# Second layer's experts: rows gathered per tile from a table in memory instead of 64 scatters into slots

## The chip, the cores and the metric

The kernel runs on one core of a Trainium2 chip. The metric is the device time of one execution in microseconds, as the median of the runs. Times inside the execution are read from a trace of one profiled execution, in microseconds from the start of its span.

## The reference, cut to what matters

The whole kernel is a chain of six layers over 16 images of 16x16 positions with 128 channels, which are 4096 tokens of 128 numbers. The change lies in the fourth of them, a mixture of 16 experts of which each token chooses two. Its hidden values are averaged over the tokens of an expert before the second weight is applied, so what the tokens of one expert need is a sum:

```python
gate_logits = x @ gate_weight.T                       # x: 4096 x 128 (normalised tokens)
top_vals, top_idx = jax.lax.top_k(gate_logits, 2)
routing_w = jax.nn.softmax(top_vals, axis=-1)
mask = jnp.any(top_idx[:, :, None] == jnp.arange(E)[None, None, :], axis=1)
h = jax.nn.silu(jnp.einsum('td,efd->tef', x, w1))     # w1: 16 x 512 x 128
counts = jnp.sum(mask, axis=0)
h_sum = jnp.einsum('tef,te->ef', h, mask.astype(h.dtype))
h_mean = h_sum / jnp.maximum(counts, 1)[:, None].astype(h.dtype)
y_mean = jnp.einsum('ef,edf->ed', h_mean, w2)
out = jnp.einsum('tk,tkd->td', routing_w, y_mean[top_idx])
```

## The kernel before, in words

The kernel is a row of stages, each a function that allocates its buffers and semaphores, runs one program per engine, and ends with a block in which GpSimd clears the stage's semaphores. All engines meet at the end of a block. A stage's program on each engine is an order written out by hand, with waits on semaphores.

`attend` runs two attention layers image by image. At its end, for each of the 16 images of the second layer, GpSimd writes the normalised tokens into `rows` (`normalise_rows`, L465), TensorE transposes them and multiplies by the gate, and VectorE copies the 16 logits of each token (L837) into `logits2`. SyncE has no program in this stage.

`route` ("route2") finds the places. VectorE picks the largest two logits of each of 32 x 128 tokens and writes 0/1 arrays of 32 x 16 elements a partition (`chosen`, L1404 to L1422), one operation waiting for the next. TensorE multiplies their sum by a triangle and by ones (L1354, L1356), which gives each token the number of tokens ahead of it in its tile and the counts of each tile. VectorE sums over the tiles by doubling steps (L1432, L1433), rounds each expert's count up to full tiles of 128, adds the starts, and gets for both choices a slot for each token (`position`, L1456 to L1458). There are at most 80 tiles of 128 slots, in an array `slots` in device memory. SyncE clears it first with 20 transfers (L1377). GpSimd then issues 64 indirect transfers (L1391), one for each choice and token tile: 128 rows of 512 bytes go from `rows` to the slots that `position` names. VectorE meanwhile finds the expert of each slot tile (`tile_expert`, L1461 to L1464) and the weights of the choices (L1468 to L1482). Beside this TensorE transposes w1 of all experts (L1293) and ScalarE copies it (L1299); they start behind the counting products.

`expert_sums` loops over the 80 slot tiles. SyncE loads four tiles with one transfer (L1517). For a tile TensorE transposes the rows (L1530), ScalarE copies them (L1539), VectorE reads the tile's expert from `tile_expert` and copies that expert's 512 columns of w1 into a ring of four (L1547, three tiles ahead), TensorE multiplies (L1558), ScalarE applies silu (L1611), VectorE sums over the 128 rows (L1621). TensorE transposes tile s+2 before it multiplies tile s. Slots that hold no token are zero, and silu of zero adds nothing to the sum. `mix_means` follows (L1663 on).

The third layer's experts use `route` again ("route3", 32 scatters at L1391), and `expert_outputs`, where GpSimd scatters one result tile at a time (L1773) and VectorE copies 1156 elements of weights a tile (also L1547). `spatial_gate`, the first stage, has GpSimd products (L230), and at its end VectorE operations on two images (L325) beside GpSimd sums (L237). GpSimd adds a bias to the tokens at the start of `attend` (L439). In `attend` TensorE also has bf16 products of 384 columns (L568).

## Time and profile before

| | us |
|---|---|
| median of 3 runs | 1054.7 (1053.21 to 1055.83) |
| the profiled execution | 1055.12 |
| its span, first to last instruction | 1053.2 |
| TensorE busy in the span | 728.9 |
| VectorE busy | 592.0 |
| ScalarE busy | 409.7 |
| GpSimd busy | 405.6 |

The busy times are sums over stages with different limits. The rows below are from the trace of the one profiled execution; its own time stands beside its span because what is worked out from the trace is compared with that execution first.

### The profile page before, as it was taken

The page shows a single profiled execution, that of the slowest core. Times are in us where ns is not written, and L with a number is a line of the kernel's source. Part 1 is how long each engine was busy: PE and PEld are TensorE (multiplying, and loading weights), DVE is VectorE, ACT ScalarE, POOL GpSimd, SP SyncE. Part 2 cuts the span into 40 slices and gives each one's busy share as a digit, 9 for nine tenths or more (in the row PEclk, how much of TensorE's full clock was granted, in tenths as well). Part 3 has the DMA queues.
Part 4 walks back from the last instruction along what each step waited for, and adds up shares of the span by engine and source line. Part 5 has one row for each costly group of instructions (what it writes and reads, how often), then busy time and mean ns, then how long its engine had stood idle before and what let it go on. Part 6 is the DMA issues. An engine that isn't in the chain of part 4 may idle for free. (4 is left out here: it accounts for less than half of the span.)

```text
span 1053.2 us, 21746 instructions
## 1 busy us (share of the span) xinstructions
PE 728.9 (69%) x7785; PEld 566.0 (54%) x7785; DVE 592.0 (56%) x1486; ACT 409.7 (39%) x801; POOL 405.6 (39%) x538
## 2 busy tenths in 40 slices
PE   1266899999999999985000299973988882019993
PEld 1124566666677777763000299951666661019982
DVE  1555567777666666645400299963566654018873
ACT  0154355565554444432000177700766651004331
POOL 0046102121257676780677200001555540744550
PEclk9977799999999999996555599956999995559995
DMA  6800000000000000006111122106000005112215
GB/s 184 278 0 1 1 2 1 2 2 2 2 2 2 2 2 2 2 2 198 41 52 52 48 61 68 42 0 180 2 1 2 2 2 101 50 50 60 56 48 159
DMA packets 58171, 46.46 MB, mean 44 GB/s; under 512 B 4579, under 2 KB 50647, under 8 KB 58083
## 3 DMA queue, kind: packets, MB, share of 16 engines
q1 hardware_dynamic: 53730, 36.86, 12.6%
q0 software_dynamic: 4352, 8.42, 2.5%
q8 instruction: 57, 0.93, 0.4%
q14 instruction: 32, 0.25, 0.1%
HBM read 26.87 MB, written 18.91 MB: 43 GB/s over the span
## 5 line engine op out<-in xcount | busy, mean ns | idle before, releaser
L781 DVE TENSOR_REDUCE attend_negmax<-ps 128x4 f32<-128x1024 f32 (+1 forms) x128 | 139.8, 1092 | 100.7 <-PE ps L521 99.8
L704 ACT ACTIVATE attend_prob<-ps 128x1024 f32<-128x1024 f32 (+1 forms) x128 | 110.6, 864 | 161.8 <-PE ps L538 161.5
L521 PE MATMUL ps<-attend_key,attend_query 32*128 32x256 f32 (+2 forms) x1024 | 130.5, 373 | 11.1 <-DVE attend_negmax L781 9.9
L538 PE MATMUL ps<-attend_query,attend_key 32*128 32x256 f32 (+2 forms) x1024 | 127.9, 345 | 0.0
L1391 POOL DMA_INDIRECT slots<-rows,position x96 | 94.3, 982 | 69.7 <-issue 52.4
L521 PEld LDWEIGHTS ps<-attend_key,attend_query 32*128 32x128 f32 x1024 | 82.6, 191 | 53.7 <-issue 48.6
L530 PE MATMUL ps<-attend_maxT,pick 32*128 32x256 f32 (+2 forms) x512 | 100.6, 389 | 0.5 <-ACT attend_prob L704 0.5
L1530 PE MATMUL ps<-const_all,sums_xs 128*128 128x128 f32 x80 | 22.3, 281 | 98.2 <-DMA sums_xs<-slots 98.1
L1547 DVE COPY sums_own<-w1T 128x512 f32 x80 | 34.1, 426 | 90.1 <-issue 84.5
L1558 PE MATMUL ps<-sums_xT,sums_own 128*128 128x128 f32 x640 | 83.4, 280 | 0.0
L1558 PEld LDWEIGHTS ps<-sums_xT,sums_own 128*128 128x128 f32 x640 | 78.9, 194 | 2.1 <-issue 1.4
L538 PEld LDWEIGHTS ps<-attend_query,attend_key 32*128 32x128 f32 x1024 | 78.2, 186 | 0.3
L1530 PEld LDWEIGHTS ps<-const_all,sums_xs 128*128 128x128 f32 x80 | 11.6, 146 | 98.9 <-DMA sums_xs<-slots 98.3
L458 POOL TENSOR_SCALAR attend_rstd<-attend_spread 128x2 f32<-128x2 f32 x32 | 7.3, 229 | 148.7 <-DVE attend_spread L831 148.7
L1773 POOL DMA_INDIRECT outputs<-expert_y,expert_token x40 | 40.9, 1023 | 50.3 <-DVE expert_y L1834 48.5
L1539 ACT ACTIVATE sums_xT<-ps 128x128 f32<-128x128 f32 x80 | 21.7, 272 | 97.7 <-PE ps L1530 97.7
L448 POOL TENSOR_SCALAR_AFFINE_SELECT attend_prob<-attend_prob 128x512 f32<-128x512 f32 x64 | 41.1, 642 | 45.9 <-ACT attend_prob L704 45.9
L591 PE MATMUL ps<-attend_prob,attend_vaug 128*32 128x256 f32 (+2 forms) x1024 | 58.3, 345 | 0.7 <-POOL attend_prob L452 0.7
L1611 ACT ACTIVATE sums_hidden<-ps 128x512 f32<-128x512 f32 x80 | 47.8, 597 | 22.1 <-DVE partial L1621 13.8
L937 POOL MEMSET linear_power<- 128x2 f32 x1 | 0.1, 100 | 143.9 <-SPq L934 143.9
L1621 DVE TENSOR_REDUCE partial<-sums_hidden 128x512 f32 (+1 forms) x80 | 54.2, 679 | 1.0 <-ACT sums_hidden L1611 0.9
L1129 ACT ACTIVATE linear_prob<-ps 128x1536 f32<-128x1536 f32 x32 | 46.1, 1441 | 15.3 <-PE ps L1021 15.3
(314 smaller groups left out, 1782.8 us busy)
## 6 DMA issues: line engine op xcount, KB each, us to landing
slots<-route_zero SPq DMA_DIRECT2D x20, 256.0 KB, 3.7
sums_xs<-slots SPq DMA_DIRECT2D x20, 256.0 KB, 2.8
w<-in_L_ffn_w SPq DMA_DIRECT2D x1, 4096.0 KB, 31.0
slots<-route_zero SPq DMA_DIRECT2D x10, 258.0 KB, 7.4
expert_xs<-slots SPq DMA_DIRECT2D x10, 258.0 KB, 2.9
x<-in_x SPq DMA_DIRECT2D x4, 512.0 KB, 9.2
experts<-in_L_ffn_W SPq DMA_DIRECT2D x1, 2048.0 KB, 8.5
experts<-in_L_ffn_W SPq DMA_DIRECT2D x4, 512.0 KB, 9.4
```

The costliest lines, as they stand in the source:

```text
L448: nc.gpsimd.affine_select(out=causal, in_=causal, pattern=[[0, 2], [0, 2], [1, 128]], base=0, channel_multiplier=-1, compare_op=ALU.is_ge, ...
L521: return nc.tensor.matmul(ps[:, SCORE + i, at:at + width], query[rows, n % 3, a * 128:(a + 1) * 128], key[rows, n % 3, odd, from_:from_ + ...
L530: nc.tensor.matmul(ps[:, KEY_SCORE + i, at:at + width], pick[rows, odd, :], maxT[rows, n % 2, from_:from_ + width], start=True, stop=False)
L538: return nc.tensor.matmul(ps[:, KEY_SCORE + i, at:at + width], key[rows, n % 3, odd, b * 128:(b + 1) * 128], query[rows, n % 3, from_:from ...
L591: mm = nc.tensor.matmul(ps[32 * r:32 * r + 32, HEADS, c:c + width], vaug[:, n % 3, b, g, r, :], of_pair(n, 2 * g + r // 2)[:, r % 2, at:at ...
L704: nc.scalar.activation(of_pair(t // 4, t % 4)[:, :, 0:wide], ps[:, KEY_SCORE:KEY_SCORE + 2, 0:wide], ACT.Exp).then_inc(prob_ready, 1)
L781: last = nc.vector.tensor_reduce(out=negmax[:, s // 4 % 2, :, r:r + 2, odd].rearrange("p a r -> p r a"), in_=ps[:, SCORE:SCORE + 2, 0:2 * ...
L1129: nc.scalar.activation(prob[:, s % 2, :, 0:384], ps[:, SCORE:SCORE + 4, 0:384], ACT.Copy).then_inc(prob_ready, 1)
L1391: nc.gpsimd.indirect_dma_start(out=slots[:, :], out_offset=bass.IndirectOffsetOnAxis(ap=position[:, k, t:t + 1], axis=0), in_=normed[:, t, ...
L1558: mm = nc.tensor.matmul(ps[:, bank + r % 2, c * 128:(c + 1) * 128], own[:, r % ring, c * 128:(c + 1) * 128], xT[:, r % 4, :], start=True, ...
L1611: nc.scalar.activation(hidden[:, r % 2, :], ps[:, UP + r % 2, :], ACT.Silu).then_inc(hidden_ready, 1)
L1621: nc.vector.tensor_reduce(out=partial[:, bass.ds(s, 1), :].rearrange("p s c -> p (s c)"), in_=hidden[:, r % 2, :].rearrange("p (c n) -> p ...
```

## The change

The scatters into `slots`, the clearing of `slots`, and the stage `route2` are gone. While `attend` runs, SyncE writes the normalised rows of each image to a `table` in device memory, behind a first row of zeros (17 transfers, the last behind the last `normalise_rows`). The stage `expert_sums` now contains the choosing too. Places are found as before, with scans (`tensor_tensor_scan`) in place of the doubling steps and with 0/1 arrays in bf16, and are split into a tile number and a lane number. In place of sending each token to its slot, the kernel finds the token of each slot: for 64 pairs of a choice and a token tile, TensorE multiplies a one-hot array of the lanes (128 x 128) by a one-hot array of the tiles (80 columns) that is scaled once by the token's number in its tile plus one (VectorE) and once by the tile's number (GpSimd). The sum over the 64 products is, for each lane and slot tile, the token's row in the table, or 0 for an empty slot. This goes in four chunks of 16 pairs with two sets of buffers. The one-hot arrays are laid into `xf` and `rows`, which are free at that point. GpSimd then issues 80 indirect transfers, one for each slot tile, that gather 128 rows of 512 bytes from the table into a ring of eight buffers, each as soon as the transpose of the tile eight earlier is done. w1 of the first eight experts is transposed before the counting products. The token numbers in the last column of `rows`, which the third layer needs, are written by VectorE in the block behind `mix_means`.

```diff
 def attend(...):
+            @block.sync
+            def _(sp):
+                sp.wait_ge(zero_row_set, 1)
+                sp.dma_start(table[0:1, :], zero_row[:]).then_inc(table_written, 16)
+                for k in range(IMAGES):
+                    sp.wait_ge(rows_ready, IMAGES + k + 1)
+                    sp.dma_start(table[1 + N * k:1 + N * (k + 1), :].rearrange("(a p) c -> p a c", p=128),
+                                 rows[:, 2 * k:2 * k + 2, 0:C]).then_inc(table_written, 16)
+                sp.wait_ge(table_written, 16 * (IMAGES + 1))
...
+def ordering(nc, sb, sem, experts, taken, tiles, given, bias, consts, tile_expert, source, ps, spare, weight,
+             counts=None, tile_choice=None, target=None):
...
+    def cast_constants(pool):
+        nc.gpsimd.tensor_tensor(before16[:], consts["before"][:], consts["ones"][:], ALU.subtract)
+        nc.gpsimd.tensor_copy(ones16[:], consts["ones"][:])
+        nc.gpsimd.tensor_copy(number16[:], consts["tile"][:])
+        nc.gpsimd.memset(restart[:], 1.0).then_inc(counts_cast, 1)
...
+    def number_tiles(pool):
+        for q in range(CHUNKS):
+            at = q % (TILES // CHUNK) * CHUNK
+            pool.wait_ge(tile_hot_ready, q + 1)
+            nc.gpsimd.tensor_tensor(numbers[:, q % 2, :, 1, :], tile_hot[:, q % 2],
+                                    over(number16[:, at:at + CHUNK, None], [128, CHUNK, tiles]), ALU.mult)\
+                .then_inc(tile_numbers, 1)
+
+    def count(pe):
+        pe.wait_ge(counts_cast, 2)
+        pe.wait_ge(chosen_ready, 1)
+        flat = select[:].rearrange("p t e -> p e t")
+        for bank, of in ((COUNT, before16), (TOTAL, ones16)):
+            mm = nc.tensor.matmul(ps[:, bank, 0:TILES * experts].rearrange("p (e t) -> p e t", e=experts), of[:],
+                                  flat, start=True, stop=True)
+        mm.then_inc(counted, 1)
+
+    def invert(pe):
+        for q in range(CHUNKS):
+            pe.wait_ge(own_numbers, q + 1)
+            pe.wait_ge(tile_numbers, q + 1)
+            for j in range(CHUNK):
+                mm = nc.tensor.matmul(ps[:, INDEX, 0:2 * tiles], lane_hot[:, q % 2, j, :],
+                                      numbers[:, q % 2, j].rearrange("p a s -> p (a s)"),
+                                      start=q == 0 and j == 0, stop=q == CHUNKS - 1 and j == CHUNK - 1)
+            mm.then_inc(inverted, 1)
...
+    def order(dve):
+        dve.wait_ge(counted, 1)
+        link(dve, nc.vector.tensor_tensor_scan(rising[:].rearrange("p e t -> p (e t)"), restart[:],
+                                               ps[:, TOTAL, 0:TILES * experts], 0.0, ALU.mult, ALU.add))
...
+        for q in range(CHUNKS):
+            k, at = q // (TILES // CHUNK), q % (TILES // CHUNK) * CHUNK
+            if q == 0:
+                dve.wait_ge(counts_cast, 2)
+            if q >= 2:
+                dve.wait_ge(inverted, q - 1)
+            nc.vector.tensor_tensor(tile_hot[:, q % 2], over(number16[:, None, 0:tiles], [128, CHUNK, tiles]),
+                                    over(tile16[:, k, at:at + CHUNK, None], [128, CHUNK, tiles]), ALU.is_equal)\
+                .then_inc(tile_hot_ready, 1)
+            nc.vector.tensor_tensor(lane_hot[:, q % 2], over(number16[:, None, :], [128, CHUNK, 128]),
+                                    over(lane16[:, k, at:at + CHUNK, None], [128, CHUNK, 128]), ALU.is_equal)
+            dve.wait_ge(tile_hot_ready, q + 1)
+            nc.vector.tensor_scalar(numbers[:, q % 2, :, 0, :], tile_hot[:, q % 2], consts["next"][:, 0:1], None,
+                                    ALU.mult).then_inc(own_numbers, 1)
+        dve.wait_ge(inverted, CHUNKS)
+        link(dve, nc.vector.tensor_copy(found[:, 0, :], ps[:, INDEX, 0:tiles]))
+        link(dve, nc.vector.scalar_tensor_tensor(out=found[:, 1, :], in0=ps[:, INDEX, tiles:2 * tiles], scalar=128.0,
+                                                 in1=found[:, 0, :], op0=ALU.mult, op1=ALU.add))
+        nc.vector.tensor_copy(source[:], found[:, 1, :]).then_inc(source_ready, 1)
...
 def expert_sums(...):
...
+            @block.gpsimd
+            def _(pool):
+                cast_constants(pool)
+                number_tiles(pool)
+                pool.wait_ge(source_ready, 1)
+                for s in range(S2):
+                    if s >= RING:
+                        pool.wait_ge(turned, s - RING + 1)
+                    nc.gpsimd.indirect_dma_start(
+                        out=xs[:, s % RING, :], out_offset=None, in_=table[:, :],
+                        in_offset=bass.IndirectOffsetOnAxis(ap=source[:, s:s + 1], axis=0))\
+                        .then_inc(loaded[s % RING], 16)
...
+                pe.wait_ge(arrived, 32)
+                turn_weights(range(8))
+                count(pe)
+                turn_weights(range(8, E2))
+                invert(pe)
+                pe.wait_ge(w1_taken, E2)
                 turn(0, 0)
                 turn(1, 1)
...
+                choose(dve)
+                order(dve)
+                dve.wait_ge(w1_taken, E2)
                 for s in range(3):
                     fetch(s, s)
+                weigh_choices(dve)
```

## Rows read from the trace of the kernel before

**Rows 1.** Windows; length, busy us (instructions), granted clock, DMA share, GB/s

```profile
core 0: us, PE busy (x) PEld busy (x) DVE busy (x) ACT busy (x) POOL busy (x), PEclk, DMA share, GB/s
...
480.00:505.00 25.00, 10.81 (x68) 8.23 (x68) 19.48 (x47) 8.18 (x17) 0.58 (x2) 0.70 0.74 210
...
505.00:595.00 90.00, 0.00 (x0) 0.00 (x0) 7.60 (x17) 0.00 (x0) 63.03 (x64) 0.50 0.14 47
...
598.00:685.00 87.00, 85.02 (x720) 82.33 (x720) 79.46 (x158) 62.79 (x161) 0.00 (x0) 0.98 0.19 56
```

**Rows 2.** Timeline, VectorE, 455 to 620; start, duration, instruction, idle time before

```profile
480.72 0.69 DVE L1404 TENSOR_REDUCE route_top<-logits 128x32 f32<-128x512 f32 x1 [2.89 <-PEq L52]
...
493.11 0.69 DVE L1429 COPY route_running<-ps 128x512 f32<-128x512 f32 x1 [3.63 <-PE ps L1356]
...
505.25 0.18 DVE L1458 CAST position<-route_slot_of 128x32 uint32<-128x32 f32 x1
...
505.34 1.48 DVE L1461 TENSOR_TENSOR route_past<-route_ends,const_all 128x1280 f32<-128x1280 f32 x1
```

**Rows 3.** Timeline, GpSimd, 455 to 620

```profile
473.77 1.58 POOL L465 TENSOR_SCALAR rows<-tokens,attend_spread,attend_rstd 128x128 f32<-128x128 f32 x2
...
506.48 1.20 POOL L1391 DMA_INDIRECT slots<-rows,position  x1 [0.30 <-issue]
...
507.98 0.97 POOL L1391 DMA_INDIRECT slots<-rows,position  x1 [0.30 <-issue]
```

**Rows 4.** Timeline, all engines, 585 to 600

```profile
586.25 0.97 POOL L1391 DMA_INDIRECT slots<-rows,position  x1 [0.30 <-issue]
...
595.24 0.94 SPq L1517 DMA_DIRECT2D sums_xs<-slots  x2
...
598.30 0.69 PE L1530 MATMUL ps<-const_all,sums_xs 128*128 128x128 f32 x2 [98.06 <-DMA sums_xs<-slots]
```

**Rows 5.** Timeline, all engines, 670 to 720

```profile
677.50 1.06 PE L1558 MATMUL ps<-sums_xT,sums_own 128*128 128x128 f32 x8
...
677.52 0.42 DVE L1547 COPY sums_own<-w1T 128x512 f32 x1
...
680.40 0.27 PE L1530 MATMUL ps<-const_all,sums_xs 128*128 128x128 f32 x1
...
684.14 0.69 DVE L1621 TENSOR_REDUCE partial<-sums_hidden 128x4 f32<-128x512 f32 x1 [0.32 <-ACT sums_hidden L1611]
...
685.96 0.63 PE L1663 MATMUL ps<-const_all,weight 128*128 128x128 f32 x4 [2.49 <-PEq L52]
```

**Rows 6.** Timeline, TensorE, 455 to 620

```profile
489.43 2.07 PE L1354 MATMUL ps<-route_select,const_all 128*128 128x512 f32 x2 [11.82 <-DVE route_select L1422]
...
599.41 1.91 PE L1558 MATMUL ps<-sums_xT,sums_own 128*128 128x128 f32 x8
```

**Rows 7.** Groups by form; busy us, mean ns of one, idle us before

```profile
L568 PE MATMUL ps<-window 128*128 128x384 bf16 x64 | 15.6, 326 | 0.0
```

**Rows 8.** Timeline, third layer's experts, 977 to 981

```profile
978.04 0.76 DVE L1547 COPY expert_own<-experts 128x1156 f32 x1 [0.67 <-DVE expert_y L1834]
...
978.15 1.50 POOL L1773 DMA_INDIRECT outputs<-expert_y,expert_token  x1 [0.91 <-DVE expert_y L1834]
```

**Rows 9.** Groups by form, GpSimd products and sums

```profile
L230 POOL TENSOR_TENSOR gate_weighted<-gate_prob,gate_xn 128x512 f32<-128x512 f32 x8 | 10.0, 1263 | 56.4 <-ACT gate_prob L195 56.4
...
L439 POOL TENSOR_TENSOR tokens<-tokens,o_bias 128x1024 f32<-128x1024 f32 x4 | 9.2, 2338 | 0.1
```

**Rows 10.** Timeline, end of the gate stage, 70 to 99

```profile
76.40 0.88 DVE L325 SCALAR_TENSOR_TENSOR gate_gated<-gate_xn,gate_small,gate_place 128x256 f32<-128x256 f32 x2 [2.53 <-ACT gate_place L208]
...
83.59 1.32 POOL L237 TENSOR_TENSOR gate_out<-gate_gated,x 128x512 f32<-128x512 f32 x1 [0.76 <-PE ps L167]
...
83.70 1.88 DVE L325 SCALAR_TENSOR_TENSOR gate_gated<-gate_xn,gate_small,gate_place 128x256 f32<-128x256 f32 x2
```

**Rows 11.** Timeline, ScalarE, 455 to 620

```profile
493.54 7.95 ACT L1299 ACTIVATE w1T<-ps 128x512 f32<-128x512 f32 x16 [3.80 <-PE ps L1293]
```

**Rows 12.** Timeline, GpSimd, 955 to 957

```profile
956.99 1.00 POOL L1773 DMA_INDIRECT outputs<-expert_y,expert_token  x1 [0.91 <-DVE expert_y L1834]
```

More of the change, by code:

```diff
@@ L331, in _, with attend @@
                             widen(b)
-def attend(nc, xf, tokens, rows, weights, consts, q_bias, key_scales, v_bias, o_bias, pick, window_mask, gate, logits,
-           ps):
+def attend(nc, xf, tokens, rows, table, weights, consts, q_bias, key_scales, v_bias, o_bias, pick, window_mask, gate,
+           logits, ps):
     ident = consts["ident"]
@@ L1565, in expert_sums @@
+def expert_sums(nc, table, spare, logits, w1_raw, w1T, arrived, tile_expert, weight, inverse, tile_choice, partial, consts,
+                ps):
+    RING = BODY
     with stage(nc, "sums") as (sb, sem):
-        xs = sb("xs", [128, 2, GROUPED, C])
+        source = sb("source", [128, S2], UINT32)
+        xs = sb("xs", [128, RING, C])
         xT = sb("xT", [128, 4, 128])
@@ L1578, in expert_sums, with turn_weights @@
         with nc.Block() as block:
-            @block.sync
-            def _(sp):
-                load_slots(sp, slots, xs, loaded, turned, S2)
+            @block.gpsimd
[10 more added lines that the diff above has]
+                        .then_inc(loaded[s % RING], 16)
             @block.tensor
             def _(pe):
-                def turn(s, r):
-                    turn_slots(nc, pe, xs, loaded, xT_ready, turned, consts["ident"], ps, TURN, s, r)
+                def turn_weights(experts):
+                    for e in experts:
+                        if e >= 4:
+                            pe.wait_ge(w1_taken, e - 3)
+                        for k in range(FC):
+                            mm = nc.tensor.transpose(ps[:, W1 + e % 4, k * 128:(k + 1) * 128],
+                                                     w1_raw[:, e * FC + k, :], consts["ident"][:])
+                        mm.then_inc(w1_turned, 1)
+                def turn(s, r):
+                    pe.wait_ge(loaded[r], 2 * s + 16 - 2 * r)
+                    if past(s, 2):
+                        pe.wait_ge(xT_ready, s - 1)
+                    nc.tensor.transpose(ps[:, TURN + r % 2, 0:128], xs[:, r, :], consts["ident"][:])\
+                        .then_inc(turned, 1)
+                pe.wait_ge(arrived, 32)
[4 more added lines that the diff above has]
+                pe.wait_ge(w1_taken, E2)
                 turn(0, 0)
@@ L1598, in _, with take_weights @@
             def _(act):
+                def take_weights(e):
+                    act.wait_ge(w1_turned, e + 1)
+                    nc.scalar.activation(w1T[:, e, :], ps[:, W1 + e % 4, :], ACT.Copy).then_inc(w1_taken, 1)
+                for e in range(E2):
+                    take_weights(e)
+                exponential(act)
                 def take(s, r):
@@ L1913, in _ @@
                 sp.wait_ge(stored, 16 * 8)
-CONSTS = {"ident": 128, "group": 128, "before": 128, "ones": 128, "index": E2, "row": 1,
-          "token": TILES, "tile": S2, "part": 128 // E2}
+CONSTS = {"ident": 128, "group": 128, "before": 128, "ones": 128, "index": E2, "row": 1, "next": 1,
+          "token": TILES, "tile": 128, "part": 128 // E2}
 def build(nc, a, out):
@@ L1967, in build @@
         inverse = sb("inverse", [128, E2])
-        slots = nc.dram_tensor("slots", (S2 * 128, C), FP32, kind="Internal").ap()
+        table = nc.dram_tensor("table", (1 + TOKENS, C), FP32, kind="Internal").ap()
         slots3 = nc.dram_tensor("slots3", (S3 * 128, C + 1), FP32, kind="Internal").ap()
@@ L2090, in build @@
         first_input.close()
-        attend(nc, xf, tokens, rows, weights, consts, q_bias, key_scale, v_bias, o_bias[:, 0, :], pick, window, gate2,
+        attend(nc, xf, tokens, rows, table, weights, consts, q_bias, key_scale, v_bias, o_bias[:, 0, :], pick, window, gate2,
                logits2, ps)
@@ L2094, in build @@
             w1T = sb("w1T", [128, E2, F], into=turning)
[L2095 to L2097 removed]
+            expert_sums(nc, table, spare, logits2, w1_raw, w1T, experts_in, tile_expert, weight2, inverse,
+                        tile_choice, partial, consts, ps)
             mix_means(nc, partial, tile_choice, w2, inverse, weight2, tokens, consts, ps)
@@ L2103, in build, with _ @@
         with nc.Block() as block:
+            @block.vector
+            def _(dve):
+                nc.vector.tensor_copy(rows[:, :, C:C + 1].bitcast(UINT32), consts["token"][:, :, None])
             @block.sync
@@ L2149, in constants @@
         "row": p.astype(np.float32),
+        "next": p.astype(np.float32) + 1,
         "token": (p + 128 * np.arange(TILES)[None]).astype(np.float32),
-        "tile": np.tile(np.arange(S2, dtype=np.float32), (128, 1)),
+        "tile": np.tile(np.arange(128, dtype=np.float32), (128, 1)),
         "part": (p // E2 == np.arange(128 // E2)[None]).astype(np.float32),
```

175 lines of the change are left out of this document (152 added, 23 removed).

## The prediction

> **What bounds the kernel now.** I read the windows by stage first, then the timelines of the engines at the edges of the second layer's expert stage, then what an indirect transfer and a GpSimd product cost elsewhere in the same trace. From 505 to 595 us the only engine that works steadily is GpSimd: TensorE and ScalarE do nothing, VectorE 7.6 of 90 us, the DMA engines 0.14 [rows 1]. In the stage behind it, 598 to 685 us, TensorE is busy 85 of 87 us. So the stretch is two walls in a row: scatters issued one by one, then a TensorE loop.
>
> VectorE chooses experts from 480.72 on, two products follow at 489.43 [rows 6], it goes on at 493.11, and has the last positions at 505.43 [rows 2]. The scatters start at the first positions, a little earlier. A scatter takes 0.97 us of GpSimd and the next starts 0.30 later, so one every 1.275 us (507.98 is the plain one) [rows 3]; the 64th begins at 586.25 and ends at 587.22, the first load of the slots is issued at 595.24, the first transpose starts at 598.30 [rows 4]. The loop's last transpose is at 680.40, so a tile takes 82.1 / 80 = 1.03 us, nearly all of it the tile's own products (1.06, overlapping the next), and its last reduction ends at 684.83 [rows 5]. From 480.72 to 684.83 is 204.1 us; this is what the change rebuilds. Every engine meets the others at a barrier ahead of it (2.89 us of idle time ahead of the choice) [rows 2] and behind it (the next stage's TensorE starts at 685.96), so each microsecond saved or lost here moves the end by as much.
>
> **The change, part by part.**
>
> *Gone:* clearing 5.2 MB of slots, 64 scatters, one stage boundary, the loop's loads from the slots. *New:* 80 gathers, issued by GpSimd one by one in the loop stage, with eight buffers; one-hot products to find each row's token ahead of the first gather; 17 writes of the table under the attention.
>
> *Table.* SyncE has no other work in the attention, and 16 of the writes lie under it. The last waits for the rows that GpSimd finishes at 475.35 (473.77 + 1.58) [rows 3], the stage ends 2.9 before 480.72, at 477.8 [rows 2]. A plain transfer here takes about 3 us from issue to use (595.24 to 598.30) [rows 4], so it lands near 478.2: 0.3 (0 to 1.5).
>
> *Choice.* The same 13 operations, 480.72 to 489.43, 8.7 us. GpSimd now casts constants beside them: three operations of 128 elements and a memset. I put 1.0 on it (0 to 2), because VectorE and GpSimd can hold each other up, as shown below. 9.7.
>
> *Counts.* Two fp32 products of 512 columns cost 3.7 us now, 489.43 to 493.11 [rows 2, 6], at a granted clock that averages 0.70 over the stretch [rows 1]. In bf16 the nearest row is 64 products of 384 columns, in pairs: 15.6 us busy, 0.49 a pair, and 0.33 for one by itself [rows 7], so the second adds 0.16. That makes 0.22 for 512 columns, 0.44 at half the clock, and 1.2 for two with the wait. Ends: 0.9 to 3.7.
>
> *Prefix and places.* Scans replace ten copies and adds. With 0.21 for each small operation and 0.72 for each of 512 elements (the spacing in rows 2), and 1.2 for the long scan, which no row shows (0.7 to 2.4): 1.2, six small, one add, one multiply-add, four for the places, six small conversions of which two overlap: 7.6. Counts and places then end at 499.3 instead of 505.4.
>
> *One-hot chunks, four of them.* VectorE: a comparison of 1280 elements, one of 2048, one scaling of 1280. The comparison of 1280 costs 1.48 [rows 2]; at 1.04 ns an element 2048 cost 2.29; the scaling, by copies of 512 in 0.42 [rows 5] and 1156 in 0.76 [rows 8], 0.82. Together 4.6. GpSimd: one product of 1280; 1.26 for 512 and 2.34 for 1024 [rows 9] give 2.1 ns an element and 2.88. Are the two beside each other? The gate stage says no: a pair of VectorE operations with two SBUF inputs takes 0.88 alone and 1.88 when a GpSimd product of 1.32 starts with it [rows 10]; one waits for the other whole. Here every VectorE operation of a chunk either has two SBUF inputs or is a two-per-cycle one. So I add them: 4 x (4.6 + 2.9) = 30.0. If they ran side by side it would be 18.4; with the scaling at one per cycle 32.6.
>
> The Trainium skill ("SBUF — State Buffer", § SBUF: two separate sides) says the same of this pair: an exclusive lock, taken for a whole instruction, against a VectorE operation in a two-port mode or with two SBUF inputs. The trace agrees: 1.88 is 0.88 and most of 1.32 in rows 10. The skill ("VectorE: DVE Perf Modes", § The perf-mode tier table) would give a bf16 tensor_tensor double rate, by which the comparisons would cost half: 7 us less and 1014 in the end, an estimate from that page; but § What auto-detection actually checks asks for a step of 1 in every tensor, and the second operand here is broadcast along its rows. No row here shows a bf16 comparison.
>
> *Inversion's tail.* Three quarters of the 64 products lie under later chunks. Of the last 16, 160 columns at half the clock are 0.14 each: 2.2, and three small VectorE operations and a wait: 3.1 in all (2 to 6).
>
> *Gathers.* 80 at the scatter's pace, 1.275: 102.0, less the last gap, 101.7. A scatter is an indirect transfer of the same 128 rows of 512 bytes, the other way round. The TensorE loop needs only 1.03 a tile, so it now waits for the gathers. What interferes: a VectorE operation that is under way as the transfer starts. The scatter at 506.48 met 0.34 of a comparison and took 0.23 longer [rows 2, 3]; the one at 978.15 met 0.65 us of a weight copy and took 0.53 longer [rows 8]. In the new loop a 0.42 copy runs every tile. If the starts fall anywhere against it, a third of them meet it, by half of it: 0.07; with the longer operations at the beginning I take 0.10 a gather, 8 in all. Ends: nothing, and 0.42 every time, which is 34.
>
> *Landing and tail.* The last scatter ends at 587.22, the next transfer is issued 8.0 later, and 2.9 of that is the stage boundary: at most 5.1 of landing. I take 2.5 (1 to 5). From the last transpose at 680.40 to the last reduction at 684.83 is 4.4 [rows 5], unchanged.
>
> *Hidden:* transposes and copies of w1 (7.95 us of ScalarE) [rows 11] start at the top of the stage, half of them under the choice and half under the prefix; without that cover they would cost up to 8. The weights of the choices, nine small operations and three of 512 elements, 4 us by the spacings above, lie under the first gathers, as do the first three weight copies. The merged stage clears some 20 more semaphores at its end; the attention's boundary (36 of them) takes 2.9, this loop's (8) 1.1, so 0.06 a semaphore and 1.3.
>
> **Sum.** 0.3 + 9.7 + 1.2 + 7.6 + 30.0 + 3.1 + 101.7 + 8 + 2.5 + 4.4 = 168.5, against 204.1: 35.6 less, with the clears 34.3. The profiled execution took 1055.1 (span 1053.2 and 1.9 around it), 0.4 above the median of the runs, 1054.7. Forecast 1020.8, said as 1021.
>
> **Rivals.**
>
> *Chunks side by side and gathers unhindered.* For it: the operands are bf16, half the bytes of those in rows 10, and the one-hot work might hold the ports less. Against it: rows 10. It gives 30.0 - 18.4 = 11.6 and 8 less: 1001.
>
> *Every gather is held by a copy.* All of the loop is paced by the gathers, so the copy keeps one phase against them, and it may be the bad one; rows 8 show the mechanism, but there the copy always starts first. A gather every 1.70: 26 more, 1046. The Trainium skill ("SBUF — State Buffer", § A bandwidth-pool intuition that's wrong) speaks against the change in this way: a GpSimd-issued transfer cannot write its descriptors while VectorE runs a two-port copy. Rows 8 agree for a copy that is under way first; no row here shows one that starts inside a transfer.
>
> *Slower than before.* One mechanism: the gather itself is dearer than the scatter, or it and the copy wait for each other. The saving of 34.3 is used up at 34.3 / 80 = 0.43 more than my 1.375, that is at 1.81 a gather. At 1.9, the pace of the third layer's loop (0.91 of idle time and 1.00 of transfer) [rows 12], it is 42 more: 1062. For it: that no row shows a gather. Against it: the scatter's 0.97 is issue work, and the direction does not change the number of rows.
>
> *No change that can be measured.* A gather between 1.77 and 1.85.
>
> **How the numbers follow.** Forecast 0.50, side by side 0.20, held by copies 0.19, slower 0.08, no change 0.03. What this kernel's measurement can tell from no change is about 0.3%, 3 us. Faster 0.89, same 0.03, slower 0.08. The forecast's own range is 1010 to 1032. The range 996 to 1046 reaches both neighbouring cases; it leaves out the last two (0.11) and the outer parts of the neighbours, 0.2 in all.
>
> **What would show it.** GpSimd idle but for four products of near 2.9 between about 499 and 529, each ending before VectorE's next operation begins; the first gather at about 532; gathers every 1.28 to 1.45, and 80 of them; TensorE waiting in the loop for the gathers' landing in every tile; the last reduction near 649. The prediction is wrong if a gather takes much over 1.0 us of GpSimd, if it lands so late that eight buffers do not cover it (over 8 us), or if TensorE, now idle for part of every tile, is granted half its clock, where a tile's products take 1.91 [rows 6] instead of 1.06 [rows 5] and would set the pace.

## The result, and the profile after

The changed kernel takes 1014.6 us (median, 1013.0 to 1017.4) where the kernel before takes 1054.0 in the same rounds: a ratio of 0.9627, 95% interval 0.9601 to 0.9653. The profiled execution took 1014.0 us, its span is 1012.1. The forecast was 1021, with 1010 to 1032 as its own range, so the direction is right and the forecast is 6 us too long.

The windows of the changed kernel by step of the rebuilt stage (columns as in [rows 1]): choice and counts, order, the four one-hot chunks, the inversion's tail, and the loop in three parts.

```profile
480.91:491.53 10.62, 8.35 (x36) 6.63 (x37) 8.16 (x14) 4.60 (x8) 1.50 (x5) 0.66 0.01 2
491.53:499.99 8.46, 6.00 (x32) 5.76 (x30) 7.91 (x18) 4.67 (x9) 0.00 (x0) 0.70 0.00 0
499.99:524.62 24.63, 6.95 (x48) 5.99 (x48) 24.62 (x12) 0.00 (x0) 17.22 (x4) 0.50 0.00 0
524.62:528.08 3.46, 2.31 (x16) 2.00 (x16) 0.98 (x4) 0.00 (x0) 0.00 (x0) 0.50 0.00 0
528.08:541.00 12.92, 7.34 (x31) 6.49 (x32) 9.68 (x22) 3.83 (x9) 10.17 (x10) 0.50 0.18 42
541.00:620.00 79.00, 71.76 (x572) 65.25 (x571) 66.28 (x128) 49.79 (x127) 60.20 (x62) 1.00 0.21 52
620.00:641.40 21.40, 15.85 (x122) 13.78 (x120) 14.85 (x27) 11.69 (x27) 8.97 (x9) 1.00 0.56 31
```

The 90 us in which only GpSimd worked [rows 1] are gone; TensorE now works while rows arrive. The last of these windows is the odd one: the DMA engines are busy 0.56 of it, against 0.21 in the window ahead, and move less (31 GB/s against 52).

Timeline of VectorE, the same edges as in [rows 2]:

```profile
488.92 0.43 DVE L1687 TENSOR_TENSOR sums_select<-sums_chosen 128x512 bf16<-128x512 bf16 x1
...
491.53 1.22 DVE L1695 TENSOR_TENSOR_SCAN sums_rising<-sums_restart,ps 128x512 f32<-128x512 f32 x1 [2.08 <-PE ps L1636]
...
495.50 1.06 DVE L1709 TENSOR_TENSOR sums_less<-sums_chosen,sums_rising 128x512 f32<-128x512 bf16 x1
...
501.40 2.28 DVE L1725 TENSOR_TENSOR xf<-sums_number,sums_lane 128x2048 bf16<-128x2048 bf16 x1
503.61 2.61 DVE L1728 TENSOR_SCALAR rows<-xf,const_all 128x1280 bf16<-128x1280 bf16 x1
506.14 1.48 DVE L1722 TENSOR_TENSOR xf<-sums_number,sums_tile 128x1280 bf16<-128x1280 bf16 x1
...
527.03 0.24 DVE L1731 COPY sums_found<-ps 128x80 f32<-128x80 f32 x1 [2.41 <-PE ps L1645]
...
527.70 1.48 DVE L1741 TENSOR_TENSOR rows<-sums_ends,const_all 128x1280 f32<-128x1280 f32 x1
```

Timeline of GpSimd, to set beside [rows 3]:

```profile
501.57 4.30 POOL L1627 TENSOR_TENSOR rows<-xf,sums_number 128x1280 bf16<-128x1280 bf16 x1 [19.09 <-DVE xf L1722]
...
528.08 2.19 POOL L1805 DMA_INDIRECT sums_xs<-table,sums_source  x1 [3.82 <-DVE sums_source L1734]
530.58 0.96 POOL L1805 DMA_INDIRECT sums_xs<-table,sums_source  x1 [0.30 <-issue]
```

Read the two together. GpSimd's product is on record for 4.30 us from 501.57 on, but VectorE's lane comparison, which started at 501.40, ends on time, at 503.68. The product ends at 505.87, and the scaling, which started at 503.61 and is on record for 2.61, ends at 506.22. Read so, each of them waits for the one before: the product works 505.87 - 503.68 = 2.19 us (no run shows it alone), the scaling 0.35. A chunk takes 506.14 - 499.99 = 6.15 us, the later ones 6.13.

Timeline of TensorE at the loop's end and at the next stage's start, to set beside [rows 5], and three groups of the stage:

```profile
619.54 0.27 PE L1825 MATMUL ps<-const_all,sums_xs 128*128 128x128 f32 x1
...
620.54 0.27 PE L1825 MATMUL ps<-const_all,sums_xs 128*128 128x128 f32 x1
...
621.64 0.33 PE L1825 MATMUL ps<-const_all,sums_xs 128*128 128x128 f32 x1
...
623.65 0.33 PE L1825 MATMUL ps<-const_all,sums_xs 128*128 128x128 f32 x1 [0.78 <-DMA sums_xs<-table,sums_source]
...
625.14 0.33 PE L1825 MATMUL ps<-const_all,sums_xs 128*128 128x128 f32 x1 [0.26 <-DMA sums_xs<-table,sums_source]
...
636.90 0.33 PE L1825 MATMUL ps<-const_all,sums_xs 128*128 128x128 f32 x1 [0.52 <-DMA sums_xs<-table,sums_source]
643.76 1.09 PE L1921 MATMUL ps<-const_all,weight 128*128 128x128 f32 x4 [3.72 <-PEq L52]
```

```profile
L1805 POOL DMA_INDIRECT sums_xs<-table,sums_source x80 | 79.3, 992 | 27.9 <-issue 20.7 <-DVE sums_source L1734 3.8 <-PE ps L1825 3.4
...
L1540 DVE COPY sums_own<-w1T 128x512 f32 x80 | 35.7, 446 | 16.7 <-issue 7.8 <-PE ps L1551 7.0 <-DVE weight L1764 0.8
L1825 PE MATMUL ps<-const_all,sums_xs 128*128 128x128 f32 x80 | 25.4, 318 | 18.1 <-DMA sums_xs<-table,sums_source 15.9 <-ACT sums_hidden L1865 1.3
```

The last gather is issued at 630.56 and done on GpSimd at 631.50, 103.4 us after the first began. The transpose of tile 70 is at 621.64; then the transposes come 1.5 to 2.0 us apart although the gathers are issued 1.25 to 1.5 apart, and the last one starts 5.4 us after its gather is done. Once TensorE has caught up with the gathers (from tile 21 on), that lag is mostly 1.5 to 1.9 us. With this input the experts' rows fill 71 tiles: 71 to 79 are wholly empty, and every empty slot asks for the same row of the table, row 0. The last tile of an expert is partly empty. Where it is mostly so, the lag is longer there too: 2.3, 2.3 and 2.5 us at tiles 51, 60 and 66, which by the choices that the reference makes on this input have 98, 101 and 114 empty slots.

### The profile page after: what moved, and what is told of

Read it like the earlier page. It is cut to its first block and busy times, and to the rows that moved or that the text cites. A ratio compares the mean times of both kernels' runs of the same rounds, so it can differ in the third digit from the quotient of the medians.

```text
span 1012.1 us, 21818 instructions
## 1 busy us (share of the span) xinstructions
PE 752.3 (74%) x7847; PEld 581.3 (57%) x7847; DVE 618.3 (61%) x1485; ACT 413.4 (41%) x801; POOL 440.6 (44%) x563
## 5 line engine op out<-in xcount | busy, mean ns | idle before, releaser
L1805 POOL DMA_INDIRECT sums_xs<-table,sums_source x80 | 79.3, 992 | 27.9 <-issue 20.7
L1551 PE MATMUL ps<-sums_xT,sums_own 128*128 128x128 f32 x640 | 86.4, 282 | 0.0
L2031 POOL DMA_INDIRECT outputs<-expert_y,expert_token x40 | 41.4, 1036 | 49.7 <-DVE expert_y L2092 48.8
L480 POOL TENSOR_SCALAR rows<-tokens,attend_spread,attend_rstd 128x128 f32<-128x128 f32 x64 | 50.6, 798 | 3.3
L973 POOL TENSOR_SCALAR_AFFINE_SELECT linear_prob<-linear_prob 128x1024 f32<-128x1024 f32 x32 | 34.9, 1092 | 38.5 <-ACT linear_prob L1144 38.5
L545 PEld LDWEIGHTS ps<-attend_maxT,pick 32*128 32x128 f32 x512 | 48.1, 184 | 1.6 <-ACT attend_prob L719 1.4
L1551 PE MATMUL ps<-expert_xT,expert_own 128*128 128x128 f32 x320 | 44.6, 285 | 0.0
```

Of the source, the lines that this page charges most:

```text
L480: last = nc.gpsimd.tensor_scalar(rows[:, t, 0:C], tokens[:, t, :], spread[:, n % 2, a, 0:1], rstd[:, n % 2, a:a + 1], ALU.subtract, ALU.mult)
L545: nc.tensor.matmul(ps[:, KEY_SCORE + i, at:at + width], pick[rows, odd, :], maxT[rows, n % 2, from_:from_ + width], start=True, stop=False)
L1551: mm = nc.tensor.matmul(ps[:, bank + r % 2, c * 128:(c + 1) * 128], own[:, r % ring, c * 128:(c + 1) * 128], xT[:, r % 4, :], start=True, ...
L1805: nc.gpsimd.indirect_dma_start(out=xs[:, s % RING, :], out_offset=None, in_=table[:, :], in_offset=bass.IndirectOffsetOnAxis(ap=source[:, ...
```

## The experiments

The kernel before took 1054.0 to 1056.0 us (median) on the chips of these runs, so times are compared by their ratio to it. The last column is the rebuilt stretch of the profiled execution, from VectorE's first choosing operation to the end of the loop's last reduction. Two executions of the changed kernel differ by 0.8 us in it. Its two ratios, 0.9627 and 0.9599, lie 0.3% apart, so a gain of under 3 us is read from the stretch and not from the time.

| run | us | ratio [95%] | stretch |
|---|---|---|---|
| changed kernel | 1014.6 | 0.9627 [0.9601, 0.9653] | 160.5 |
| the same again | 1011.9 | 0.9599 [0.9576, 0.9623] | 161.3 |
| 128 zero rows | 1011.1 | 0.9581 [0.9552, 0.9611] | 155.9 |
| one row for all | 1041.3 | 0.9856 [0.9829, 0.9882] | 187.5 |
| plain loads | 996.9 | 0.9435 [0.9405, 0.9464] | 142.8 |
| no weight copy | 1010.1 | 0.9562 [0.9539, 0.9586] | 158.6 |
| product on VectorE | 1009.7 | 0.9566 [0.9541, 0.9591] | 157.5 |
| scaling on ScalarE | 1010.0 | 0.9561 [0.9533, 0.9590] | 155.8 |
| comparison moved | 1012.2 | 0.9589 [0.9562, 0.9616] | 160.2 |
| choices by expert | 1014.4 | 0.9603 [0.9575, 0.9630] | 160.7 |
| sums written across | 1013.6 | 0.9606 [0.9584, 0.9628] | 159.9 |
| combined | 1002.1 | 0.9508 [0.9480, 0.9535] | 150.5 |

### Late transfers: 128 zero rows, and one row for all

```diff
-                sp.dma_start(table[0:1, :], zero_row[:]).then_inc(table_written, 16)
+                sp.dma_start(table[0:128, :], zero_row[:]).then_inc(table_written, 16)
...
-        nc.vector.tensor_copy(source[:], found[:, 1, :]).then_inc(source_ready, 1)
+        link(dve, nc.vector.tensor_scalar(found[:, 0, :], found[:, 1, :], 0.0, consts["back"][:, 0:1],
+                                          ALU.is_equal, ALU.mult))
+        nc.vector.scalar_tensor_tensor(out=source[:], in0=found[:, 1, :], scalar=127.0, in1=found[:, 0, :],
+                                       op0=ALU.add, op1=ALU.add).then_inc(source_ready, 1)
```

(`back` is the partition less 127, so partition p reads zero row p, and token rows start at 128.)

> Theory: the late transfers come from empty slots, which all ask for the one zero row of the table (with this routing tiles 71 to 79 are wholly empty). With 128 zero rows, one for each partition, the wait of TensorE for a tile after its gather stays at the 1.5 to 1.9 us of the full tiles up to the last, instead of growing to 5.4: the last transpose comes 3.5 us earlier, against 0.2 to 0.3 us for the one more operation ahead of the first gather. Time about 1011, gathers still 1.25 to 1.3 us apart. Rival: transfers lag because some eighty have been queued by then, whatever they read: the lag at tile 79 stays above 4 us and the time is 1014 to 1015.

The counterpart makes every slot ask for row 0:

```diff
-        nc.vector.tensor_copy(source[:], found[:, 1, :]).then_inc(source_ready, 1)
+        nc.vector.tensor_scalar(source[:], found[:, 1, :], 0.0, None, ALU.mult).then_inc(source_ready, 1)
```

> Every slot asks for row 0, so the experts work on zeros; nothing else changes. Theory of the shared row: what was seen over the empty tiles 71 to 79, transposes 1.5 to 2.0 us apart, now holds from the first tile to the last: 80 tiles at 1.5 to 2.0 us, so 16 to 56 us more, 1030 to 1070 us. Rival (transfers lag through their number, not their address): the spacing stays at 1.3 us and the time at 1014 to 1015.

Windows with 128 zero rows (the loop's end), then TensorE's last transpose there:

```profile
620.00:636.00 16.00, 14.81 (x115) 13.02 (x113) 13.04 (x25) 9.91 (x25) 8.26 (x9) 1.00 0.14 41
```

```profile
632.18 0.29 PE L1828 MATMUL ps<-const_all,sums_xs 128*128 128x128 f32 x1
```

Window and gathers with one row for all:

```profile
541.00:620.00 79.00, 59.51 (x433) 50.13 (x432) 53.09 (x98) 40.93 (x97) 48.61 (x51) 1.00 0.90 40
```

```profile
L1805 POOL DMA_INDIRECT sums_xs<-table,sums_source x80 | 77.7, 971 | 50.7 <-PE ps L1825 41.4 <-issue 5.5 <-DVE sums_source L1734 3.8
```

With the empty slots spread, the DMA engines are busy 0.14 of the loop's end, 620 to 636, where the changed kernel's are busy 0.75 of the same window. The last transpose comes at 632.18, 1.5 us after its gather is done, and the stretch is 4.6 us shorter. Tiles 51, 60 and 66 gain too: 1.6, 1.5 and 1.7 us after their gathers. With one row for all the DMA engines are busy 0.90 of the loop at 40 GB/s, GpSimd waits 41.4 us for a buffer to be read, and the stretch is 27.0 us longer, 0.34 a tile. The two theories' numbers were far apart, and both runs fell to the shared row. 128 reads of one row are slow in the DMA engines; that the transfers lag through their number is ruled out. What in the engines or the memory makes them slow, no run here shows.

### What the gathers cost the loop: plain loads in their place

```diff
+            @block.sync
+            def _(sp):
+                sp.wait_ge(source_ready, 1)
                 for s in range(S2):
                     if s >= RING:
-                        pool.wait_ge(turned, s - RING + 1)
-                    nc.gpsimd.indirect_dma_start(
-                        out=xs[:, s % RING, :], out_offset=None, in_=table[:, :],
-                        in_offset=bass.IndirectOffsetOnAxis(ap=source[:, s:s + 1], axis=0))\
-                        .then_inc(loaded[s % RING], 16)
+                        sp.wait_ge(turned, s - RING + 1)
+                    at = s % TILES * 128
+                    sp.dma_start(xs[:, s % RING, :], table[at:at + 128, :]).then_inc(loaded[s % RING], 16)
```

> SyncE loads 128 rows of the table in their order for each tile, after the same wait on the indices, so the experts get unsorted rows; the gathers are gone. Theory: the loop goes at the pace of the 80 gathers on GpSimd (1.30 us each). Without them VectorE's copy and reduction bind, 0.45 + 0.68 = 1.13 us a tile, after some 13 us in which TensorE's products still take 1.91 us: the last transpose near 625 instead of 636.9, and with no empty tile's transfer late the time is about 1003. Rival: the loop is bound by VectorE or TensorE already, or by the transfers themselves: 1012 to 1015.

Window of the loop, and two transposes of TensorE:

```profile
541.00:620.00 79.00, 76.48 (x661) 74.05 (x660) 74.13 (x150) 56.33 (x147) 0.00 (x0) 1.00 0.19 55
```

```profile
598.08 0.27 PE L1827 MATMUL ps<-const_all,sums_xs 128*128 128x128 f32 x1
...
599.08 0.27 PE L1827 MATMUL ps<-const_all,sums_xs 128*128 128x128 f32 x1
```

The gathers do bind: without them the stretch is 17.7 us shorter. That holds the 4.6 us of the shared row too, as each plain load reads 128 different rows. The floor I had expected was wrong. I had added VectorE's recorded 0.45 and 0.68 to 1.13 a tile; it is 1.00, near TensorE's pace in [rows 5]. Durations of neighbours on one engine overlap in the records: here VectorE's copy at 597.23 is on record for 0.43, and the reduction behind it starts at 597.58. Pace is read from starts, not from sums of durations. VectorE's copies come 0.99 us apart (597.23, 598.22), so this run does not tell which of the two engines binds the loop without gathers.

### What stretches a gather: no weight copy, and the comparison moved

From the fifth tile on the first run copies 8 columns of the weights instead of 512. Its own line stands in place of the call of `fetch_weights`, which copies `own[:, r % ring, :]`:

```diff
-                    fetch_weights(nc, dve, w1T, own, 4, tile_expert, up_done, own_ready, s, r)
+                    if isinstance(s, int) and s < 4:
+                        return fetch_weights(nc, dve, w1T, own, 4, tile_expert, up_done, own_ready, s, r)
...
+                    nc.vector.tensor_copy(own[:, r % 4, 0:8], w1T[:, bass.ds(e, 1), 0:8].rearrange("p a f -> p (a f)"))\
+                        .then_inc(own_ready, 1)
```

> From the fifth tile on VectorE copies 8 columns of the expert's weights instead of 512, so the products use wrong weights. Theory: the copies are what stretches some gathers over 0.94 us. Then the copies that meet a gather are gone, nearly all 79 later gathers take 0.94 to 0.95 us against a mean of 0.98 now: 2 to 3 us in all, time about 1012. Rival 1: copies do not touch gathers: mean 0.98 as before, 1014.6. Rival 2: VectorE's time per tile binds the loop as much as the gathers do; then the loop gains more than 4 us.

```profile
L1805 POOL DMA_INDIRECT sums_xs<-table,sums_source x80 | 77.0, 962 | 27.9 <-issue 19.8 <-PE ps L1825 4.3 <-DVE sums_source L1734 3.8
```

The row is the group of its gathers. Less the first one of 2.19, the mean is (77.0 - 2.19) / 79 = 0.947 against (79.3 - 2.19) / 79 = 0.976 in the changed kernel: 2.3 us in all, and the stretch is 1.9 shorter. So the copies are what stretches the later gathers, and little. The time, 1010.1, is 4.5 us under the first median of the changed kernel and 1.8 under the second; that VectorE's time binds the loop as well, the second rival, finds no support in the stretch.

The second run moves the stage's long comparison (line 1741) ahead of the wait for the last products:

```diff
+        shape = [128, tiles, experts]
+        link(dve, nc.vector.tensor_tensor(past, over(end[:, None, :], shape),
+                                          over(consts["tile"][:, 0:tiles, None], shape), ALU.is_le))
         dve.wait_ge(inverted, CHUNKS)
...
-        shape = [128, tiles, experts]
-        link(dve, nc.vector.tensor_tensor(past, over(end[:, None, :], shape),
-                                          over(consts["tile"][:, 0:tiles, None], shape), ALU.is_le))
```

> The comparison of tiles with experts' ends (two inputs in SBUF, 1.48 us) moves into VectorE's idle 2.41 us ahead of the last products. Theory (this comparison held the first gather): the first gather takes 0.95 to 1.1 us instead of 2.19, and the loop starts 1.1 us earlier; the second and later ones as before. Rival (the first gather of the stage is slow in itself): it stays at 2.2 us and nothing is gained.

```profile
526.97 1.22 POOL L1805 DMA_INDIRECT sums_xs<-table,sums_source  x1 [3.89 <-DVE sums_source L1737]
```

The first gather takes 1.22 instead of 2.19, a little more than the 0.95 to 1.1 expected: the comparison had held it. The stretch gains 0.3 us over one execution of the changed kernel and 1.1 over the other, so of the 1.0 us no more can be said than that it may arrive at the end.

### Who waits for whom in a chunk

The tile-number product on VectorE:

```diff
+            nc.vector.tensor_tensor(numbers[:, q % 2, :, 1, :], tile_hot[:, q % 2],
+                                    over(number16[:, at:at + CHUNK, None], [128, CHUNK, tiles]), ALU.mult)\
+                .then_inc(tile_numbers, 1)
...
-                number_tiles(pool)
```

> The tile-number product moves from GpSimd to VectorE, behind the scaling. Theory (GpSimd's product waits until VectorE's lane comparison ends and then holds the scaling back): the 2.61 us on record for the scaling is some 0.35 of work and 2.2 of waiting. Without GpSimd a chunk is 1.49 + 2.28 + 0.35 + 1.49 = 5.6 us instead of 6.13, 2.1 us less over four chunks. Rival (the two engines work side by side and the scaling really takes 2.61): a chunk is 1.49 + 2.28 + 2.61 + 1.49 = 7.9 us, 7 us more over four chunks.

One chunk on VectorE's timeline, from its lane comparison on:

```profile
500.83 2.28 DVE L1725 TENSOR_TENSOR xf<-sums_number,sums_lane 128x2048 bf16<-128x2048 bf16 x1
503.04 0.55 DVE L1728 TENSOR_SCALAR rows<-xf,const_all 128x1280 bf16<-128x1280 bf16 x1
503.50 1.48 DVE L1730 TENSOR_TENSOR rows<-xf,sums_number 128x1280 bf16<-128x1280 bf16 x1
504.90 1.48 DVE L1722 TENSOR_TENSOR xf<-sums_number,sums_tile 128x1280 bf16<-128x1280 bf16 x1
```

The same, with ScalarE for the scaling by the token's number (VectorE's scaling goes, the product as above):

```diff
+            act.wait_ge(tile_hot_ready, q + 1)
+            nc.scalar.activation(numbers[:, q % 2, :, 0, :], tile_hot[:, q % 2], ACT.Copy,
+                                 scale=consts["next"][:, 0:1]).then_inc(own_numbers, 1)
...
-            nc.vector.tensor_scalar(numbers[:, q % 2, :, 0, :], tile_hot[:, q % 2], consts["next"][:, 0:1], None,
-                                    ALU.mult).then_inc(own_numbers, 1)
```

> ScalarE scales by the token's number while VectorE compares lanes, VectorE makes the tile-number product; GpSimd has no part in the chunks. Theory: ScalarE does not hold VectorE, so a chunk is VectorE's 1.49 + 2.28 + 1.49 = 5.3 us, 3.5 us less than now over four chunks, with ScalarE's operation (1280 elements, near 1.4 us by its 0.60 us for 512) hidden behind the lane comparison. Rival: any second engine that reads the same buffers stretches VectorE's operations: comparison of lanes over 3 us, no gain.

ScalarE's and VectorE's timelines:

```profile
502.42 1.36 ACT L1634 ACTIVATE rows<-xf,const_all 128x1280 bf16<-128x1280 bf16 x1 [3.33 <-DVE xf L1728]
```

```profile
502.30 2.28 DVE L1731 TENSOR_TENSOR xf<-sums_number,sums_lane 128x2048 bf16<-128x2048 bf16 x1
504.50 1.48 DVE L1734 TENSOR_TENSOR rows<-xf,sums_number 128x1280 bf16<-128x1280 bf16 x1
```

The scaling that was on record for 2.61 takes 0.55 once GpSimd is out, so most of the 2.61 was waiting. A chunk takes 5.47 us on VectorE alone and 5.01 with ScalarE, against 6.13; from the first comparison to the first gather it is 25.5 and 23.6 us against 28.1. The lane comparison takes 2.28 with ScalarE at work on the same buffer and 2.28 without, so of these two engines only GpSimd makes VectorE wait here. Both rivals fall. GpSimd as a helper made the chunks slower than VectorE by itself.

### The order in memory: two ways to count

First, VectorE stores the choices expert by expert, so that TensorE reads one run, and the running counts are written once in token order:

```diff
-        flat = select[:].rearrange("p t e -> p e t")
+        flat = select[:]
...
-            nc.vector.tensor_tensor(select[:], chosen[0][:], chosen[1][:], ALU.add).then_inc(chosen_ready, 1)
+            nc.vector.tensor_tensor(select[:].rearrange("p e t -> p t e"), chosen[0][:], chosen[1][:], ALU.add).then_inc(chosen_ready, 1)
...
-        link(dve, nc.vector.scalar_tensor_tensor(out=rising[:], in0=over(start[:, :, None], by_expert), scalar=128.0,
+        link(dve, nc.vector.scalar_tensor_tensor(out=scratch[:].rearrange("p t e -> p e t"), in0=over(start[:, :, None], by_expert), scalar=128.0,
```

> The choices are stored expert by expert, so TensorE reads its 512 columns in one run, and the running counts are written once in token order instead of read twice across it. Theory: order of the operand costs TensorE half its rate: the two counting products take 0.45 to 0.55 us each instead of 1.08 and 1.10 (1.1 us less), and VectorE's two products with the counts 0.7 instead of 1.06 and 1.04 (0.7 less), against 0.2 to 0.6 for the sum written across and 0.3 for the counts written across: 0.5 to 1.3 us less. Rival: 1.08 is what 512 columns cost at this clock however they lie; then only the terms of VectorE move, and the gain is under 0.3 us.

VectorE, then TensorE:

```profile
490.26 2.38 DVE L1687 TENSOR_TENSOR sums_select<-sums_chosen 128x512 bf16<-128x512 bf16 x1
```

```profile
493.00 0.38 PE L1636 MATMUL ps<-sums_select,sums_ones 128*128 128x512 bf16 x1 [5.00 <-DVE sums_select L1687]
493.21 1.15 PE L1817 MATMUL ps<-const_all,w_raw 128*128 128x128 f32 x5
```

Second, the choices stay as they were, TensorE reads one run and writes across PSUM; the running counts are written once in token order as in the first:

```diff
-            mm = nc.tensor.matmul(ps[:, bank, 0:TILES * experts].rearrange("p (e t) -> p e t", e=experts), of[:],
+            mm = nc.tensor.matmul(ps[:, bank, 0:TILES * experts].rearrange("p (e t) -> p t e", e=experts), of[:],
```

> The choices stay stored token by token, as VectorE writes them in 0.43 us; TensorE reads them in one run and writes its 512 sums across PSUM instead. Theory: the order of the operand that TensorE reads is what halves its rate, not the order of what it writes, so the two products take 0.2 to 0.5 us each as when the choices lay expert by expert, and the first scan starts 1.0 to 1.4 us earlier; with the counts written across once (1.07 us for 0.69, then 0.69 twice for 1.06 and 1.04) 0.3 us more: 1.3 to 1.7 us in all, before the first gather. Rival: writing across costs TensorE as much as reading across: the products stay near 1.1 us and only 0.3 us is gained.

```profile
491.27 1.14 PE L1636 MATMUL ps<-sums_select,sums_ones 128*128 128x512 bf16 x1 [3.12 <-DVE sums_select L1687]
```

In the first run the two products take 0.77 us from the end of the sum to the scan, against 2.18 in the changed kernel. The part about TensorE was right in direction, but two things moved at once: the second product takes 0.21 us to the next start at a granted clock of 1.00, against 0.92 in the changed kernel at 0.50. A factor of two of that is the clock, the other 2.2 the order. But VectorE's sum, written across in bf16, takes 2.38 us instead of 0.43, far over the 0.2 to 0.6 that I had allowed, and the whole gains nothing. In the second run the products stay at 2.05 us: its rival was right, writing across costs TensorE about as much as reading across (0.86 us to the next start, 491.27 to 492.13, at a granted clock of 0.53). The 0.3 to 0.4 us that stay are VectorE's multiplications, 0.69 us instead of 1.06 when their operand lies in a run. Neither time can be told from the changed kernel's.

### All that gained, together

128 zero rows, ScalarE and VectorE for the chunks, the comparison moved, sums across PSUM:

> All edits that gained, together: 128 zero rows, ScalarE for the token's number and VectorE for the tile's, the comparison with the experts' ends ahead of the last products, sums written across PSUM. Theory: the gains stand one after the other on the same path and add up: transfers of empty slots 3.5 to 4.5, chunks 4.4, first gather 1.0, counts 1.3 to 1.7, so 10 to 11.5 us, near 1004 where the changed kernel takes 1014.6. Rival: in the loop the bound moves to the gathers' issue (80 at 1.25 us) whatever is done there, and the clock of TensorE rises later after a shorter stage, so that part of it is lost: 1007 to 1009.

> The changed kernel once more, as the reference for the two others on this chip: 0.9627 of the kernel before, 1014 to 1017 us.

1002.1 us against 1011.9 for the changed kernel in the same rounds, so 9.8 less; the intervals of the ratios do not touch. The stretch is 10.0 us shorter than the first execution's: 0.5 ahead of the chunks, 4.0 from there to the first gather, 5.5 in the loop. That is just under the 10 to 11.5 expected. The gains stand one after the other and add up, nearly in full. This kernel is faster than the kernel before and than the changed one.

## Why the prediction was right, step by step

The prediction's sum for the stretch was 168.5 us; measured are 160.7 (with the 0.2 us by which it starts later). Its terms, in their order (all from the one profiled execution):

- **Table** 0.3: 0.2, the choice starts at 480.91 instead of 480.72. The second execution starts it at 479.54, so 0.2 says no more than that the table costs little.
- **Choice** 9.7: 8.6, 480.91 to 489.50. Of the 1.0 us for GpSimd's casts beside it nearly nothing came.
- **Counts** 1.2: 2.0. The 0.22 us for 512 columns came from a row whose columns lie in a run. Here TensorE reads them across, and that cost twice as much at the same half clock (0.92 to the next start for the 0.44 taken); inside the bounds of 0.9 to 3.7.
- **Prefix and places** 7.6: 8.5. The long scan took 1.22, as taken; the two multiplications that read the counts across took 1.06 and 1.04 instead of 0.69.
- **Chunks** 30.0: 24.6, the largest miss. The step that decided, one engine behind the other, is right and shown by two runs. Three sizes were off: GpSimd's product is 2.19 and not 2.88 (rows of fp32 products gave 2.1 ns an element, a bf16 one takes 1.7), the scaling 0.35 to 0.55 and not 0.82, and neighbours on VectorE overlap by 0.08 each, which a sum of durations counts twice.
- **Inversion's tail** 3.1: 3.5.
- **Gathers** 101.7 and 8 for interference: 103.4 together. A gather alone is 0.945 and not 0.97, so 80 at 1.25 less a gap are 99.7. Interference is 3.7: 1.2 of it the first gather, the rest, 2.5, the copies, 0.03 a gather instead of 0.10. A copy that holds every gather was not seen; whether that is a matter of their phase was not tried.
- **Landing** 2.5: 1.6 for a full tile, 5.4 for the last, outside the bounds of 1 to 5. This term held a mechanism that I had not seen. It was costed from the distance between two stages of the kernel before, whose loads read each row once, and says nothing of 128 reads of one row. With 128 zero rows the last lag is 1.5 and the stretch 4.6 us shorter.
- **Tail** 4.4: 4.5. **Clears** 1.3: 1.2 (643.76 - 641.40 = 2.4, against 1.1 before).

The misses have both signs. Table, choice, chunks and gathers were put 12.9 us too high, counts, places, inversion's tail, landing and tail 5.1 too low. So the mechanisms carry the forecast, but part of its closeness is luck: the shared row, which it did not foresee, brings the time nearer to it. With 128 zero rows the time is 1011.1, near the lower end of the range. Two rivals and one sign are a little off the prediction's own terms: 1020.8 + 26 is 1047 and not 1046, 1020.8 + 42 is 1063 and not 1062, and counts and places would end at 499.5 and not 499.3; nothing hangs on them.

That leaves 1.7 us by which the next stage got longer. Its first four products take 1.09 instead of 0.63, at a granted clock of 0.50 from 643.76 to 646.00. In the second execution of the changed kernel TensorE idled just as long ahead of them, and they take 0.63:

```profile
643.21 0.63 PE L1921 MATMUL ps<-const_all,weight 128*128 128x128 f32 x4 [3.72 <-PEq L52]
```

From these products to the third layer's first it is 48.0 us in the kernel before, 49.7 here and 48.9 in that second execution. So about half of the 1.7 belongs to this one execution, in which the clock was lower, and why it was stays open. The whole of the profiled execution is 1055.1 - 43.4 + 1.2 + 1.7 - 0.6 for all other stages = 1014.0.

Of the signs that I had named, the four products between 499 and 529 are there, though each ends inside VectorE's next record and not ahead of it, as that record contains the wait. Gathers come every 1.30 us. TensorE waits for a transfer in 38 of the 80 tiles (25 of the products and 34 of the weight loads wait), not in every one: it starts the loop at half its clock, at 1.9 us a tile until about 541 (granted clock 0.50 in the window), falls behind, and then catches up at 1.00 a tile. The rule of the Trainium skill on the exclusive lock ("SBUF — State Buffer", § SBUF: two separate sides) agrees with the chunks' records and with 0.55 for 2.61. Of the rule on double rate ("VectorE: DVE Perf Modes", § What auto-detection actually checks), both halves are seen: 512 bf16 elements with a step of 1 take 0.43 us (line 1687), 1280 with a broadcast operand 1.48, no less than in fp32. The 1014 that the double rate would have given is what was measured, but by chance: the comparisons took 1.48 and 2.28, as the forecast had them.

Of the rivals, side by side (1001) came true in one half, gathers nearly unhindered, and fell in the other; held by copies (1046) and slower than before are out, the gather at a mean of 1.30 where the latter began at 1.81.

## What to carry to other kernels

If a gather needs a place for empty slots, do not give it one row for all: 128 zero rows, one for each partition, cost 0.3 us of VectorE and saved 4.6 in all; numbers between 1 and 128 were not tried. Before work is put on GpSimd "beside" VectorE, look in the trace whether one record contains the other's wait; ScalarE was free and did not collide. And where an operand has to be turned in memory, cost the turn on each side, the write as well as the read, from a row with that stride.

## What the runs showed of the hardware beyond that

- 128 reads of one row of 512 bytes occupy the DMA engines far longer than 128 of different rows: busy share 0.90 at 40 GB/s, against 0.21 at 52.
- Access across costs each engine: VectorE's bf16 write 2.38 us for 0.43, its fp32 read 1.06 for 0.69, its fp32 write about the same (1.07); TensorE's second counting product 0.92 us to the next start at a granted clock of 0.50 (490.39 to 491.31), against 0.21 in a run at 1.00 (493.00 to 493.21, choices by expert). The clock's two levels explain a factor of two of that, the order the rest. The Trainium skill ("SBUF — State Buffer", § Door 1: The DMA port swizzle) states short lines of 16 bytes in SBUF and 8 in PSUM, past which strides cost; the runs agree in direction, and no run here measures a line's length.
- A gather takes GpSimd 0.945 us, a scatter of the same rows 0.97 [rows 3].
